# A graph layer on one core: degrees from 16-bit row sums, the exponentials' tail on another engine, one more unit of distance

## The reference, cut to what matters

```python
# x: (8192, 128) fp32; adj: (8192, 8192) of zeros and ones, about one in a thousand set
h = maximum(layernorm(x), 0)
deg = clip(adj.sum(axis=1), 1.0)
dis = deg ** (-0.5)
diffusion = dis[:, None] * adj * dis[None, :] @ h - h
sim = h @ h.T / (norms[:, None] * norms[None, :])
attn = softmax(beta * sim * adj, axis=1)
out = x + diffusion + sigmoid(alpha) * (attn @ h - h)
```

## Time and profile before

| what | value |
|---|---|
| median of 3 runs | 2115.04 us (2114.71 to 2115.41) |
| the profiled execution | 2113.9 us, its span 2112.1 us |
| mean granted TensorE clock | 0.994 of full speed |
| busy share of the span | PE 92%, PEld 72%, DVE 71%, ACT 61%, POOL 10% |
| attention loop, first product to last | 145.6 to 1637 us |
| diffusion stage | 1652.7 to 2112 us |

### The profile page before, as it was taken

How to read it: one execution, slowest core, us unless ns; L and a number is a source line. 1 busy time by engine, 2 the same in 40 slices (tenths; PEclk the granted TensorE clock), 3 DMA queues, 4 the chain that set the end, 5 groups by cost and what they waited for, 6 DMA issues and landing times.

```text
span 2112.1 us, 52471 instructions
## 1 busy us (share of the span) xinstructions
PE 1945.4 (92%) x23682; PEld 1520.1 (72%) x23682; DVE 1504.4 (71%) x1563; ACT 1298.6 (61%) x1267; POOL 221.2 (10%) x276
## 2 busy tenths in 40 slices
PE   0139999999999999999999999999999799999998
PEld 0127777777777777777777777777777688888887
DVE  4678998999998999899988989999998311111110
ACT  3638888888888888888888888888887400000000
POOL 1560001000000110000011000000100000000000
PEclk9999999999999999999999999999999899999999
DMA  7157666777666677766667777666752644544440
GB/s 143 69 109 100 91 82 95 94 100 93 94 91 81 93 93 97 98 96 82 90 90 93 93 101 99 81 91 81 98 82 114 256 161 162 180 180 171 156 164 11
DMA packets 179700, 229.88 MB, mean 109 GB/s; under 512 B 8340, under 2 KB 155796, under 8 KB 174228
## 3 DMA queue, kind: packets, MB, share of 16 engines
q0 software_dynamic: 135168, 67.13, 39.8%
q1 hardware_dynamic: 26644, 151.01, 18.7%
q10 hardware_dynamic: 17664, 8.39, 1.5%
HBM read 348.13 MB, written 79.69 MB: 203 GB/s over the span
## 4 chain that ended last, share of the span: by engine, by line
PE 90%; ACT 4%; DVE 4%; DMA 1%; issue 0%; SPq 0%; ACTq 0%; DVEq 0%
PE cos_ps L549 30%; PE top_ps L570 12%; PE top_ps L574 11%; PE cos_ps L599 11%; PE top_ps L572 11%; PE top_ps L599 11%; PE top_ps L561 4%; ACT arena L275 1%; ACT xe L293 1%; DMA asb<-x_in 1%; DVE vc L378 1%; DVE elo L471 1%; DVE ssq L413 1%; ACT ehi L326 0%; ACT xe L330 0%
## 5 line engine op out<-in xcount | busy, mean ns | idle before, releaser
L326 ACT ACTIVATE ehi<-xe,ebias,ab 128x1024 f16<-128x1024 f32 x512 | 635.4, 1241 | 266.0 <-DVE xe L465 265.7
L570 PE MATMUL top_ps<-h,ehi 128*128 128x129 f16 x4096 | 719.2, 220 | 10.1 <-DVE elo L471 7.1
L574 PE MATMUL top_ps<-h,elo 128*128 128x129 f16 x4096 | 718.6, 220 | 0.0
L572 PE MATMUL top_ps<-hlo,ehi 128*128 128x128 f16 x4096 | 717.7, 219 | 0.0
L465 DVE TENSOR_TENSOR xe<-cos_ps,arena 128x1024 f32<-128x1024 f32 x512 | 622.0, 1215 | 123.9 <-issue 70.0
L471 DVE TENSOR_TENSOR elo<-xe,ehi 128x1024 f16<-128x1024 f32 x512 | 622.4, 1216 | 22.8 <-ACT xe L330 6.5
L330 ACT ACTIVATE xe<-xe,ebias,ab 128x1024 f32<-128x1024 f32 x512 | 628.4, 1227 | 0.0
L570 PEld LDWEIGHTS top_ps<-h,ehi 128*128 128x128 f16 x4096 | 399.0, 97 | 21.2 <-DVE elo L471 7.9
L574 PEld LDWEIGHTS top_ps<-h,elo 128*128 128x128 f16 x4096 | 400.0, 98 | 0.0
L572 PEld LDWEIGHTS top_ps<-hlo,ehi 128*128 128x128 f16 x4096 | 399.8, 98 | 0.0
L549 PE MATMUL cos_ps<-uT_hi 128*128 128x512 f16 x1024 | 305.0, 380 | 1.4 <-DVE uT_lo L431 1.3
(11 more groups left out here) (77 smaller groups left out, 1228.7 us busy)
## 6 DMA issues: line engine op xcount, KB each, us to landing
arena<-adj_in_dram POOLq DMA_DIRECT2D x256, 256.0 KB, 16.1
at_scratch<-arena SPq DMA_DIRECT2D x128, 512.0 KB, 4.8
arena<-at_scratch SPq DMA_DIRECT2D x24, 2048.0 KB, 8.0
xe<-at_scratch SPq DMA_DIRECT2D x8, 2048.0 KB, 7.9
asb<-x_in SPq DMA_DIRECT2D x16, 256.0 KB, 10.9
h_scratch<-arena SPq DMA_DIRECT2D x4, 1024.0 KB, 3.9
base_scratch<-asb SPq DMA_DIRECT2D x4, 1024.0 KB, 5.0
arena<-h_scratch SPq DMA_DIRECT2D x1, 4096.0 KB, 14.4
```

The costliest lines, as they stand in the source:

```text
L326: nc.scalar.activation(ehi[:, n % ES, :], xm[:, n % XS, :], ACT.Exp, bias=ebias[:, 0:1], scale=ab[:, 1:2]).then_inc(ehi_done, 1)
L570: nc.tensor.matmul(top_ps[:, bank, col:col + P + 1], head, h1[:, s, 0:P + 1], start=(first and t % 3 == 0), stop=final, skip_group_check=True)
L572: nc.tensor.matmul(top_ps[:, bank, col:col + P], head, hlo[:, s, :], start=False, stop=final, skip_group_check=True)
L574: last = nc.tensor.matmul(top_ps[:, bank, col:col + P + 1], tail, h1[:, s, 0:P + 1], start=False, stop=final, skip_group_check=True)
```

## The change

- `sums` loses its 8 products for the degrees. VectorE adds up the loaded rows instead (`sum_rows`): it reads two bytes as one 16-bit integer, 1024 of them in an instruction, into PSUM, 8 instructions for each chunk of 16 units. Once a panel, `sum_bytes` takes low and high bytes apart (4 small instructions). At the end `degrees` adds across partitions with 8 fp32 products of 32 columns on TensorE, ahead of `sums(511)`, and VectorE copies the result (`copy_deg`).
- `rest(n)` moves from VectorE to GpSimd, whose list now also holds the loads of the rows, one DMA after each of eight units.
- `sums` runs three units behind `cosines` (LAG), with four slots for `ehi` and `elo`, which take the place of `ustage`.
- A third slot for the rows (RS); the slots of the diffusion stage become five, and their first loads wait for other things: the first for the stores alone, the second for `x_done`, the third for `elo_done`. The fetch of `h` (L207) waits for the row sums.

```diff
-    XS, ES = 2, 3
+    XS, ES = 2, 4
+    LAG = 3
+    RS = 3
+    EIGHT = 56
+    PAIR = 256 * EIGHT
+    MAGIC = 1.5 * 2.0 ** 23
...
-        deg_ps = top_ps[:, 3, 0:PT]
-        ab_ps = top_ps[:, 3, 16:18]
+        ab_ps = top_ps[:, 3, 0:2]
+        pairs_ps = top_ps[:, 3, 0:256]
+        upper_ps = top_ps[:, 3, 256:512]
+        deg_ps = top_ps[:, 3, 0:256].rearrange("p (q s) -> p q s", q=Q)
...
+        ehi = ustage[:, 0:2048].bitcast(fp16).rearrange("p (s i) -> p s i", s=ES)
+        elo = ustage[:, 2048:4096].bitcast(fp16).rearrange("p (s i) -> p s i", s=ES)
...
-        slots = [arena[:, 0:4096], xe[:, :], arena[:, 4096:8192], arena[:, 8192:12288]]
+        h_again = arena[:, 2 * 4096:4 * 4096].rearrange("p (s d) -> p s d", d=P)
+        slots = [arena[:, 4096:8192], arena[:, 0:4096], xe[:, :], arena[:, 8192:12288], arena[:, 12288:16384]]
...
+            sp.wait_ge(rows_summed, 8 * CHUNKS)
             sp.wait_ge(h_kept, 16 * CH)
             sp.dma_start(h_again.rearrange("p s d -> p (s d)"), h_dram).then_inc(h_back, 16)
             for w in range(W):
                 sp.wait_ge(at_stored[w], 16 * CHUNKS)
             for k in range(CHUNKS):
-                if k == 0:
-                    sp.wait_ge(attn_done, UNITS)
+                if k == 1:
+                    sp.wait_ge(x_done, UNITS)
                 elif k == 2:
+                    sp.wait_ge(elo_done, UNITS)
+                elif k == 3:
                     sp.wait_ge(y_scaled, PANELS)
...
+            def load_rows(k, part):
                 w0, b = panel_of(k // CH)
-                ch = k % CH
-                for q in range(Q):
-                    for w in range(2):
-                        pool.dma_start(rows8[k % 2][C * q:C * (q + 1), 16 * w:16 * (w + 1), :],
-                                       adj_v[b, w0 + w][:, :, 2048 * ch + 512 * q:2048 * ch + 512 * (q + 1)]
-                                       ).then_inc(rows_loaded[k % 2], 16)
-            load_rows(0)
+                ch, q, w = k % CH, part // 2, part % 2
+                pool.dma_start(rows8[k % RS][C * q:C * (q + 1), 16 * w:16 * (w + 1), :],
+                               adj_v[b, w0 + w][:, :, 2048 * ch + 512 * q:2048 * ch + 512 * (q + 1)]
+                               ).then_inc(rows_loaded[k % RS], 16)
+            for part in range(8):
+                load_rows(0, part)
+            for part in range(8):
+                load_rows(1, part)
...
-            load_rows(1)
-            for k in range(2, CHUNKS):
-                pool.wait_ge(at_ready, W * (k - 1))
-                load_rows(k)
+            def rest(n):
+                pool.wait_ge(ef_done, n + 1)
+                if n >= ES:
+                    pool.wait_ge(attn_done, n - ES + 1)
+                nc.gpsimd.tensor_tensor(elo[:, n % ES, :], ef[:, n % XS, :], ehi[:, n % ES, :], ALU.subtract).then_inc(elo_done, 1)
+            for part in range(8):
+                load_rows(2, part)
+            for n in range(UNITS):
+                rest(n)
+                part, k = (n - 13) % 16, (n - 13) // 16 + RS
+                if n >= 13 and part < 8 and k < CHUNKS:
+                    if part == 0:
+                        pool.wait_ge(rows_summed, 8 * (k - RS + 1))
+                        pool.wait_ge(at_ready, W * (k - RS + 1))
+                    load_rows(k, part)
...
-                w0, b = panel_of(panel)
-                nc.scalar.activation(deg[:, :].rearrange("p (ch w b) -> p w ch b", w=W, b=B)[:, w0:w0 + 2, :, b],
-                                     deg_ps.rearrange("p (w ch) -> p w ch", w=2), ACT.Copy).then_inc(acc_copied, 1)
+                    last = nc.scalar.activation(asb[:, t0 + 3 * k:t0 + 3 * k + n, 0:P + 1],
+                                                top_ps[:, k, 0:n * HS].rearrange("p (t d) -> p t d", d=HS)[:, :, 0:P + 1], ACT.Copy)
+                last.then_inc(acc_copied, 1)
...
-                if n % TILES == 1 and n > TILES:
+                if n % TILES == LAG - 1 and n > TILES:
...
+            def sum_rows(k, part):
+                if part == 0:
+                    dve.wait_ge(rows_loaded[k % RS], 16 * 8 * (k // RS + 1))
+                of = slice(64 * (k % CH) + 8 * part, 64 * (k % CH) + 8 * (part + 1))
+                nc.vector.tensor_reduce(out=pairs_ps[:, of], in_=rows_pairs[k % RS][:, 8 * part:8 * (part + 1), :],
+                                        axis=AX.X, op=ALU.add).then_inc(rows_summed, 1)
+            def sum_bytes(panel):
+                dve.wait_ge(rows_summed, 8 * CH * (panel + 1))
+                link(nc.vector.tensor_scalar(upper_ps, pairs_ps, 1.0 / PAIR, MAGIC - 1.0 / 1024, ALU.mult, ALU.add))
+                link(nc.vector.tensor_scalar(upper, upper_ps, MAGIC, 255.0 * EIGHT, ALU.subtract, ALU.mult))
+                link(nc.vector.tensor_tensor(bytesums, pairs_ps, upper, ALU.subtract))
+                nc.vector.tensor_reduce(out=rowsums[:, 32 * panel:32 * (panel + 1)],
+                                        in_=bytesums.rearrange("p (ch a h) -> p a ch h", ch=CH, h=2),
+                                        axis=AX.XY, op=ALU.add).then_inc(rowsums_ready, 1)
+            def copy_deg():
+                dve.wait_ge(deg_done, 1)
+                for q in range(Q):
+                    last = nc.vector.tensor_copy(deg[C * q:C * (q + 1), :], deg_ps[C * q:C * (q + 1), q, :])
+                link(last)
...
-            def rest(n):
-                dve.wait_ge(ef_done, n + 1)
-                if n >= ES:
-                    dve.wait_ge(attn_done, n - ES + 1)
-                nc.vector.tensor_tensor(elo[:, n % ES, :], ef[:, n % XS, :], ehi[:, n % ES, :], ALU.subtract).then_inc(elo_done, 1)
             dve.wait_ge(h_kept, 16 * CH)
             dve.wait_ge(hlo_ready, CH)
             dve.wait_ge(base_ready, CH)
             turn(0)
             copy_uT(3)
+            sum_rows(0, 0)
             for n in range(UNITS):
-                if n % B == 2 and n // B + 1 < BLOCKS:
+                masked(n)
+                if n % B == 1 and n // B + 1 < BLOCKS:
                     turn(n // B + 1)
-                masked(n)
-                if n >= 1:
-                    rest(n - 1)
-            rest(UNITS - 1)
-            dve.wait_ge(acc_copied, PANELS)
-            nc.vector.tensor_scalar(va[:, :], deg[:, :], 1.0, None, ALU.max).then_inc(deg_ready, 1)
+                elif n % B == 3 and n + 1 < UNITS:
+                    sum_rows((n + 1) // 16, 2 * ((n + 1) % 16 // B))
+                elif n % B == 0:
+                    sum_rows(n // 16, 2 * (n % 16 // B) + 1)
+                if n % TILES == TILES - 2:
+                    sum_bytes(n // TILES)
+            copy_deg()
...
+            def degrees():
+                pe.wait_ge(same_ready, 1)
+                pe.wait_ge(rowsums_ready, PANELS)
+                rows_v = rowsums.rearrange("p (v b w ch q) -> p v q ch w b", v=2, b=B, w=2, ch=CH)
+                deg_v = deg_ps.rearrange("p q (ch v w b) -> p v q ch w b", ch=CH, v=2, w=2)
+                for q in range(Q):
+                    for v in range(2):
+                        last = nc.tensor.matmul(deg_v[:, v, q], same_c[:, :], rows_v[:, v, q], start=(q == 0 and v == 0),
+                                                stop=True, skip_group_check=True)
+                last.then_inc(deg_done, 1)
             def sums(n):
                 s = tile_of(n % TILES // 16, n % 16 // B, n % B)
                 first, final = n % TILES == 0, n % TILES == TILES - 1
                 if first and n:
                     pe.wait_ge(acc_copied, n // TILES)
-                pe.wait_ge(at_ready, n // B + 1)
-                for t in range(PT):
-                    nc.tensor.matmul(deg_ps[:, t:t + 1], at8[:, n // B % W, t * P:(t + 1) * P, n % B], onesb[:, :],
-                                     start=(first and t == 0), stop=final, skip_group_check=True)
+                if n == UNITS - 1:
+                    degrees()
                 pe.wait_ge(elo_done, n + 1)
...
-            for n in range(UNITS + 2):
+            for n in range(UNITS + LAG):
                 if n < UNITS:
                     cosines(n)
-                if n >= 2:
-                    sums(n - 2)
+                if n >= LAG:
+                    sums(n - LAG)
```

More of the change, by code:

```diff
@@ L62, in sem @@
             return ctx.enter_context(nc.semaphore(name))
-        arena = sb("arena", [P, 3 * 4096], fp32)
+        arena = sb("arena", [P, 4 * 4096], fp32)
         uT_hi = sb("uT_hi", [P, N], fp16)
@@ L69, in gnn_block_kernel @@
         xe = sb("xe", [P, 4096], fp32)
-        ehi = sb("ehi", [P, ES, PW], fp16)
-        elo = sb("elo", [P, ES, PW], fp16)
         asb = sb("asb", [P, TILES, HS], fp32)
@@ L77, in gnn_block_kernel @@
         ones32 = sb("ones32", [1, P], fp32)
-        onesb = sb("onesb", [P, 1], bf16)
+        same_c = sb("same_c", [P, P], fp32)
         ab_row = sb("ab_row", [1, 2], fp32)
@@ L87, in gnn_block_kernel @@
         gz = sb("gz", [P, TILES], fp32)
```

(17 more changed lines are left out.)

23 lines of the change are left out of this document (12 added, 11 removed).

## The result

The changed kernel takes 1987.88 us (median of 4 runs, 1986.97 to 1989.30) against 2114.88 us of the kernel before in the same runs: a ratio of 0.940, 95% interval 0.9385 to 0.9417. The forecast was 1985, its own range 1977 to 1993 and the range for eight cases in ten 1976 to 2015. The profiled execution took 1987.21 us, its span 1985.4.

A forecast was written before the change was run, and what follows sets the result against it. TensorE was taken as the bound, 2.64 us per loop unit; the loop ends 131.5 us earlier, scaling 1.5 later, so 2113.9 becomes 1983.9, median 1985 us. Own range 1977 to 1993, eight in ten 1976 to 2015.

The forecast's parts named there:

- The bound: Attention loop: TensorE sets the pace; without 0.21 us of degree products a unit takes 1.29 + 1.35 = 2.64 us.
- The 2 us that I kept for boundaries: Attention loop: of 4.8 us lost before between unit sum and measured span, 2 were kept in the forecast.
- VectorE: Attention loop: mask, quarter transpose and half a row sum take 1.16 + 0.31 + 0.57 = 2.04 us per unit.
- Rival 3: Attention loop: VectorE stays second bound because integer row sums run at half rate, delaying masks; 1995 to 2015 us; 6%.
- GpSimd: Attention loop: subtraction takes 1.96 us, an issue 0.66; 2.70 us per unit with issue, 2.04 without, 2.37 on average.
- No contention: Attention loop: VectorE's remaining operations, none with two SBUF inputs, run beside GpSimd's subtraction without being held up.
- rival 2: Attention loop: VectorE and GpSimd exclude each other, a unit at least 3.12 us, about 2230 us or 2400 with issues; 7%.
- The distance: Attention loop: chain mask, head, ef, tail takes 6.0 us; sums come 7.9 us after at three units, slack 1.9.
- the stall: Attention loop: 0.17 us lost in every fourth unit by late sums; claimed to have no cause after the change.
- Panel ends: Panel ends in the loop: ScalarE's copies no longer hold TensorE; 3 of 3.7 us of weight-load waits go.
- The tail: Loop's end after the last cosines: last sums and fp32 degree products (2.4 us), ending 8.5 us later; bounds 7.4 to 10.7.
- Between the stages: From loop to diffusion stage: scaling of h starts later by 1.5 us than the 10.85 before; bounds -5.5 and +5.

The follow-up runs named there:

- root first: Changed kernel with base loads issued behind the scaling of h, degree products ahead of sums(510), root and scaling ahead of the last copy of sums: 1978.20 us.
- the extra operation: Changed kernel with one more 128-column subtraction on GpSimd behind each subtraction, which nobody waits for: 2066.36 us.
- the run with two SBUF inputs: Changed kernel with each VectorE row sum replaced by an equally long fp16 addition reading two SBUF tiles, degrees left out: 2149.24 us.

## Why the prediction was right, point by point

- **The bound.** TensorE's sums and cosines are the loop's period, measured 2.65 against the 2.64 of the sum. That 0.01 is what missed: 1346.3 against 508 x 2.64 = 1341.1 is 5.2 us, of which the panel ends explain about 1 (0.13 each, the first 0.19) and the rest, 508 x 0.008, is what the rounding of 1.29 + 1.35 leaves: the mean unit is 2.648. The 2 us that I kept for boundaries covered part of it. The cosines end at 1500.60, not 1497.3: 3.3 us, the whole difference between 1983.9 and the 1987.21 of the profiled execution. Everything behind that point came out within 0.3. The first sums at 154.29, forecast 154.2, are in part luck: in the two kernels that change only what comes after the loop they start at 154.67 (base loads behind the scaling) and 155.37 (root first).
- **VectorE.** A row sum occupies it for 1.14 us from start to start (1.15 taken), so the integer input goes at the pace of fp32; a unit is 2.10 us, not 2.04. Rival 3 had no ground.
- **GpSimd.** The subtraction took 2.14 us (2.10 from its start to the next), not 1.96: half the columns took more than half of the 3.92 in the earlier trace rows. That it would be half "if it has no fixed part" was the condition I had named. The issue took 0.67 as taken. The unit with an issue was 2.77, not 2.70, and the mean 2.44, not 2.37. The step was mis-sized by 0.07 and hidden: eight units fall 8 x 0.12 = 1 us behind, under the 1.7 us of slack below. By the figure of the Trainium skill's GPSIMD Engine Reference ("Performance versus the Vector engine") I had set 2.25 beside it; the trace lies between 1.96 and 2.25, and the extra operation shows what another 0.37 would have cost.
- **No contention.** Masks stayed at 1.225 us and rival 2 did not happen; the run with two SBUF inputs shows it was the form of the operations that avoided it. The conclusion was right, but my rows didn't carry it: the operation held there (L413) has one SBUF input, like the reciprocal that passed, so they don't tell inputs apart. The same timeline of the kernel before has an operation with two SBUF inputs that was held beside L249:

```profile
84.22 3.49 DVE L378 TENSOR_TENSOR vc<-vc,ssq 128x16 f32<-128x16 f32 x1
```

  Right behind it, still beside L249 (83.98 to 89.42), one of the same form (L379, at 87.75) took 0.17. So the set-up doesn't settle the question, and for the forms of the loop the run with two SBUF inputs does.

- **The distance.** The chain is 6.2 us (6.0 taken; from the end of `cosines(510)`, 1500.60 - 2.65, to its sums at 1504.11), the slack 3 x 2.65 - 6.2 = 1.7. That the stall would go was right, the reason given wasn't the whole of it: the prediction put it to VectorE's lighter list. The distance by itself removes it with that list unchanged, 27 us. Whether the lighter list would have done it too, no run separates.
- **Panel ends.** I let 3 of 3.7 us go, expecting ScalarE's copies to stop holding TensorE. They did not stop. This row of waits of the changed kernel answers to the earlier trace rows:

```profile
PEld top_ps L640 <- ACT asb L346: 3.2, 7, 0.5
```

  A greater distance doesn't remove this wait, because `sums` of a new panel writes where the copy still reads, whatever lies between mask and sums. This step was wrong; on PE it is the 0.13 us per panel end above, about 1 us in all.
- **The tail.** First sums 154.29 (154.2). `sums(510)` starts 3.51 after the cosines' end (3.36), the degree products take 1.75 (2.4 taken, 0.4 to 4.6 bounds; 1505.48 to 1507.23), and the loop ends (the last copy's start) 8.2 after the cosines (8.5).
- **Between the stages.** 12.45 us from the sums' end to the scaling, 12.35 taken (10.85 + 1.5). Moving the loads shows that this was held by the issue: without it the scaling comes 7.7 us earlier and the median falls by 6, where I had -5.5 as the bound below. That the sum of the traffic (10 MB at 4 MB in 10.5 us) gave the right time doesn't show that the traffic is the cause; the first two DMAs speak for something more.
- **What carried the gain.** The forecast added TensorE's 0.21 us and the stall and did not say how little of the first is to be had without the second. The runs show it: 27 and 29 alone, 113 together, 127 with the subtraction on GpSimd, although the row sums then have to be paid for.

## What to carry to other kernels

When one engine sets the pace and the next is close behind, relieving the first is worth only what the second and the pipeline's distance leave: price the parts together, and look for the pattern over several units, not at one. Test a pipeline's distance D as (chain from the end of one stage to the release of the next, plus one unit's own work) / (D + 1) against the unit's period: if it is longer, it is the period (2.95 against 2.65, measured 2.94), but if it is shorter, that isn't enough (2.62 against 2.65, measured 2.84, where by the argument above a block's turn makes one tail in four late). Before moving an operation to GpSimd, look at what stays on VectorE beside it: one form exchanged for another of equal length cost 161 us here, and every DMA issue in GpSimd's list counts in its unit.

## What the runs showed of the hardware

- The exclusion between the two engines isn't bounded by one operation of the other. VectorE's addition waited for three subtractions in a row, 6.68 us for a 1.21 us operation; 2.48 us was the mean of all.
- GpSimd's subtraction doesn't halve with its columns: from start to start 3.90 us for 2048 columns (80.08 to 83.98) and 2.10 for 1024. A line through these two has an estimated 0.3 us at zero columns and 0.53 at 128, where a subtraction with fp16 inputs took 0.37; so the fixed part isn't pinned down.
- Of four DMAs issued in a row on ScalarE's queue the first two took 0.60 and 0.67 us and the last two 10.94 together, where the same four behind the scaling took 0.60 to 0.65 each; a compute instruction behind them in ScalarE's list waits as long (9.72 us of idle time before L385).
